# First attention of a two-layer transformer kernel: the fine scores move behind the second values product

## The chip, the cores and the metric

The kernel runs on one core of one Trainium2 chip. Times are device microseconds (us) from the first to the last instruction of that core, as the median of several executions; one profiled execution gives the rows below. PE is TensorE (PEld its weight loads), DVE is VectorE, ACT is ScalarE, POOL is GpSimd, SP is SyncE, which issues most of the DMAs.

## The reference

Two pre-norm layers over 4096 tokens of width 256; only the first attention matters here. Layer norm, three projections, 16 heads of width 16, softmax over all 4096 positions, and an output projection:

```python
def _L0_attn_ref(x, Wq, bq, Wk, bk, Wv, bv, Wo, bo):
    q = _split_heads(x @ Wq.T + bq)
    k = _split_heads(x @ Wk.T + bk)
    v = _split_heads(x @ Wv.T + bv)
    scores = jnp.einsum('hbnd,hbmd->hbnm', k, q) * SCALE
    attn = jax.nn.softmax(scores, axis=-1)
    out = jnp.einsum('hbnm,hbmd->hbnd', attn, v)
    out = jnp.moveaxis(out, 0, 2).reshape(x.shape[0], x.shape[1], DIM)
    return out @ Wo.T + bo
```

Rows of the score matrix belong to keys, the softmax runs over the queries, and the result has one row for each key. Behind it come a two-expert feed-forward layer, a linear attention and a 64-expert mixture, none of which the change touches.

## The kernel before, in words

The function `attention_phase` computes the first attention. Heads go in 8 pairs (`HPAIRS`), two heads beside each other on partitions 0 to 63 and 64 to 127. For each pair the 4096 key columns go in 8 blocks of 512 (`NB`), so there are 64 turns (pair, block), and in a turn the 4096 queries go in 32 chunks of 128 (`MC`).

PE makes four kinds of product, each in a helper:

- `units_a` (line 771): raw scores, keys against 512 queries at a time, both heads, into one of two pairs of banks of `A`. DVE takes the maximum of each (line 882, `PM<-A`). They run one block and 10 units ahead, since a turn's scores need its maxima. It waits for DVE to have emptied the bank pair.
- `unit_s` (line 784): one chunk of one head, 128 queries x 512 keys, with the negated maximum added by extra rows, into one of three banks of `SB`. ACT takes the exponential (line 859, `PR<-SB`).
- `unit_fine` (line 792): the same for the second head's odd chunks, of bf16 parts with 99 rows, as four products of 32 columns, into one bank of `SB`.
- `values` (line 804): `PR` of one chunk, both heads, times the values `VH`, accumulated over the turn in `PV`: four products, each run as two passes of 256 columns, so eight records.

Score number v = 2c + e of a turn (chunk c, head e) takes bank `s_bank(v)`. `unit_s` and `unit_fine` wait until ACT has read what the bank held before (`s_before(v)`). In the rule this is score v - 3; only at the start of a turn the bank order restarts, and score 4 waits for score 3, the one just ahead of it.

PE's function `step` writes one turn out by hand, as 16 iterations of two chunks (q = 2, 4, ..., 32); the scores run two chunks ahead of the values. The order within an iteration is: `units_a`, `unit_s` three times (scores 2q, 2q+1, 2q+2), `units_a`, `values(q-2)`, `unit_fine` (score 2q+3), `values(q-1)`. The third `unit_s`, score 2q+2, waits for the exponential of score 2q-1, which is the preceding iteration's fine score. `values(q-1)` needs that same exponential; `unit_fine` needs the exponential of score 2q.

ACT's function runs `exp` over scores in their order (each waits until PE has made it, and every second one until `values` has freed the buffer of `PR`, of which there are eight), and at a turn's end, behind the exponentials of the next turn's scores 0 to 3, copies `PV` to `OS` (line 870). DVE does the maxima alone, 32 a turn, and one reduction of them. POOL splits the negated maxima into parts, rearranges the keys and issues the stores of `OS`. SP loads keys and queries and places the maxima's parts as rows of `KST` and `KF`. Semaphores count events: `s_done` for finished scores, `s_free` for finished exponentials, `p_free` for finished `values`, `a_done` and `a_free` for raw scores.

Of the kernel before, what the change touches and what calls it, by code (L numbers as in the profile page):

```python
# [112 lines left out]
def count(events):  # L113


    return events + FIRST
# [478 lines left out]
def s_bank(v):  # L595

    return (v if v < 4 else v + 2) % S_BANKS


def s_before(v):  # L600

    for w in range(v - 1, v - EXPS, -1):
        if s_bank(w % EXPS) == s_bank(v):
            return w
# [41 lines left out]
def attention_phase(nc, d, K, V_all, QST, QF):  # L646
# [5 lines left out]
    with ExitStack() as ctx:  # L652
# [35 lines left out]
        def in_steps(eng, body):  # L688

            with eng.Fori(0, HPAIRS // 2) as two:  # L690
                for hp in range(2):
                    for nb in range(NB):
                        body(two, hp, nb)

        def number(two, hp, nb):
            return two * (2 * NB) + (hp * NB + nb)

        sem.start()
        with nc.Block() as block:
# [65 lines left out]
            @block.tensor  # L765
            def _(pe):
                def unit_a(u, e, nb, slot):
                    i, j = divmod(u, NB)
                    rows = slice(e * HALF, e * HALF + STACK)
                    keys = KA[rows, nb % K_SLOTS, i * P:(i + 1) * P]  # L770
                    return nc.tensor.matmul(A[:, u % 2 * 2 + e, :], keys, QST[rows, slot, j * TB:(j + 1) * TB],  # L771
                                            start=True, stop=True)

                def units_a(b, u, nb, slot):
                    pe.wait_ge(a_free, count(b * MC + (u + 1)))
                    first = u % 2
                    unit_a(u, first, nb, slot)
                    unit_a(u, 1 - first, nb, slot).then_inc(a_done, 1)

                def unit_s(t, c, e, nb, slot):  # L780
                    v = 2 * c + e
                    rows = slice(e * HALF, e * HALF + ROWS)
                    pe.wait_ge(s_free, count(t * EXPS + (s_before(v) + 1 + S_BANKS)))
                    nc.tensor.matmul(SB[:, s_bank(v), :], QST[rows, slot, c * P:(c + 1) * P],  # L784
                                     KST[rows, nb % K_SLOTS, :], start=True, stop=True).then_inc(s_done, 1)

                def unit_fine(t, c, nb, slot):
                    v = 2 * c + 1
                    pe.wait_ge(s_free, count(t * EXPS + (s_before(v) + 1 + S_BANKS)))
                    for r in range(4):  # L790
                        at = c // 2 * P + r * 2 * HD
                        mm = nc.tensor.matmul(SB[r * 2 * HD:(r + 1) * 2 * HD, s_bank(v), :],  # L792
                                              QF[0:FINE_ROWS, slot, at:at + 2 * HD],
                                              KF[0:FINE_ROWS, nb % K_SLOTS, :], start=True, stop=True)
                    mm.then_inc(s_done, 1)

                def values(t, c, slot):
                    if c == 0:
                        pe.wait_ge(pv_read, count(t))
                    pe.wait_ge(s_free, count(t * EXPS + (2 * c + 2 + S_BANKS)))  # L800
                    for e in range(2):
                        for b in range(2):
                            at = HALF * e + 2 * HD * b
                            mm = nc.tensor.matmul(PV[at:at + 2 * HD, 0:HB], VH[:, slot, e, c, :],  # L804
                                                  PR[:, (2 * c + e) % P_SLOTS, b * HB:(b + 1) * HB],
                                                  start=(c == 0), stop=(c == MC - 1))
                    mm.then_inc(p_free, 1)

                def step(two, hp, nb):
                    t = number(two, hp, nb)  # L810
                    for q in range(2, MC + 2, 2):
                        ahead, u = divmod(q + LEAD, MC)
                        ahead += 1
                        past, a_nb = divmod(nb + ahead, NB)
                        a_slot = 1 - hp if past else hp
                        if u == 0:
                            pe.wait_ge(ka_ready, count((t + (ahead + 1)) * 2))
                            if a_nb == 0:
                                pe.wait_ge(q_loaded[1 - hp], count((two + (hp + 1) // 2 + 1) * Q_LOAD))
                        s_t, s_nb, s_slot = t, nb, hp  # L820
                        if q >= MC:
                            s_t, s_nb, s_slot = t + 1, (nb + 1) % NB, 1 - hp if nb == NB - 1 else hp
                        if q == MC:
                            block = hp * NB + nb + 1
                            pe.wait_ge(shift_loaded[s_nb % 2], count((two * 8 + (block // 2 + 1)) * SHIFT))
                        units_a(t + ahead, u, a_nb, a_slot)
                        unit_s(s_t, q % MC, 0, s_nb, s_slot)
                        unit_s(s_t, q % MC, 1, s_nb, s_slot)
                        unit_s(s_t, q % MC + 1, 0, s_nb, s_slot)
                        units_a(t + ahead, u + 1, a_nb, a_slot)  # L830
                        if q == 2 and nb == 0:
                            pe.wait_ge(vh_ready, count(two * 4 + (hp * 2 + 2)))
                        values(t, q - 2, hp)
                        unit_fine(s_t, q % MC + 1, s_nb, s_slot)
                        values(t, q - 1, hp)

                pe.wait_ge(q_loaded[0], count(Q_LOAD))
                pe.wait_ge(ka_ready, count(2))
                for u in range(MC):
                    units_a(0, u, 0, 0)  # L840
                pe.wait_ge(ka_ready, count(4))
                for u in range(LEAD):
                    units_a(1, u, 1, 0)
                pe.wait_ge(shift_loaded[0], count(SHIFT))
                units_a(1, LEAD, 1, 0)
                unit_s(0, 0, 0, 0, 0)
                unit_s(0, 0, 1, 0, 0)
                unit_s(0, 1, 0, 0, 0)
                units_a(1, LEAD + 1, 1, 0)
                unit_fine(0, 1, 0, 0)  # L850
                in_steps(pe, step)

            @block.scalar
# [1354 lines left out]
```

## Time and profile before

| what | value |
|---|---|
| median of 3 runs | 4705.39 us |
| lowest and highest run | 4700.58, 4717.93 us |
| span of the profiled execution | 4704.8 us |
| copies of `PV` at the ends of its first and last turn | 305.2 and 2770.9 us |
| PE busy (matmuls) | 4447.2 us, 95% |
| DVE busy | 3534.6 us, 75% |
| ACT busy | 3123.8 us, 66% |
| POOL busy | 853.4 us, 18% |

Besides its span no time of its own is listed for the profiled execution. Busy shares are averages over stages with different limits. Matmuls are pipelined and their recorded ends are modelled, so a busy PE is not PE at its peak; what an engine waited for, and when the next instruction could start, says more.

### The profile page before, as it was taken

The numbers are of one execution on the slowest core, as the hardware profiler recorded it, in microseconds if no ns is written. First come the engines' busy times: TensorE is split into PE (matmuls) and PEld (weight loads), VectorE is DVE, ScalarE is ACT, GpSimd is POOL, SyncE is SP. The second block draws the span as 40 slices with busy tenths as digits, with TensorE's granted clock in tenths as the row PEclk, the third lists the DMA queues.
The fourth block names the chain that finished last, engine by engine and source line by source line (L and its number), as shares of the span: only waits on it lengthen the run. The fifth ranks groups of instructions, "written<-read, shape, count | busy, mean of one in ns | idle before, by whom it ended". The sixth has DMA issues, their size and how long they took to land. (4 is left out here: it accounts for less than half of the span.)

```text
span 4704.8 us, 108333 instructions
## 1 busy us (share of the span) xinstructions
PE 4447.2 (95%) x36787; PEld 2714.8 (58%) x36787; DVE 3534.6 (75%) x3673; ACT 3123.8 (66%) x5610; POOL 853.4 (18%) x1747
## 2 busy tenths in 40 slices
PE   6599999999999999999999969999987699999999
PEld 5344444444444444444444437777866578888887
DVE  4499999999999999999999966555444564545554
ACT  3168888888888888888888855444455454444444
POOL 4311122122111222111211210000000022222222
PEclk8789999999999999999999989999998799999999
DMA  4410110100100101002111130010010422222222
GB/s 160 138 29 13 24 19 13 30 14 13 30 13 18 26 13 30 13 13 66 40 40 40 40 104 27 19 36 27 5 41 27 150 81 87 83 80 86 86 86 87
DMA packets 225729, 229.03 MB, mean 49 GB/s; under 512 B 129665, under 2 KB 169265, under 8 KB 224193
## 3 DMA queue, kind: packets, MB, share of 16 engines
q1 hardware_dynamic: 183936, 146.41, 12.5%
q0 software_dynamic: 41344, 76.61, 5.3%
q8 instruction: 286, 4.69, 0.4%
q14 instruction: 163, 1.33, 0.1%
HBM read 174.41 MB, written 64.55 MB: 51 GB/s over the span
## 5 line engine op out<-in xcount | busy, mean ns | idle before, releaser
L882 DVE TENSOR_REDUCE PM<-A 128x2 f32<-128x1024 f32 x2092 | 2455.3, 1220 | 127.0 <-PE A L771 93.4
L859 ACT ACTIVATE PR<-SB 128x512 f32<-128x512 f32 x4100 | 2121.8, 602 | 374.1 <-PE SB L784 354.5
L804 PE MATMUL PV<-PR,VH 128*32 128x256 f32 x16384 | 1298.5, 387 | 8.1 <-issue 8.1
L771 PE MATMUL A<-QST,KA 48*128 48x512 f32 x4184 | 1196.3, 476 | 59.9 <-DMA QF<-QFD 33.9
L804 PEld LDWEIGHTS PV<-PR,VH 128*32 128x32 f32 x16384 | 434.1, 110 | 562.9 <-issue 374.2
L771 PEld LDWEIGHTS A<-QST,KA 48*128 48x128 f32 x4184 | 430.1, 187 | 521.1 <-issue 413.1
L784 PE MATMUL SB<-KST,QST 50*128 50x512 f32 x3075 | 689.0, 411 | 0.4 <-issue 0.3
L784 PEld LDWEIGHTS SB<-KST,QST 50*128 50x128 f32 x3075 | 388.4, 187 | 205.9 <-ACT PR L859 201.4
L792 PE MATMUL SB<-KF,QF 99*32 99x512 bf16 x4100 | 417.3, 385 | 1.2 <-ACT PR L859 1.2
L2095 DVE TENSOR_TENSOR m_h_lo<-m_h,m_h_hi 128x512 fp32r<-128x512 f32 x320 | 221.2, 691 | 257.3 <-ACT m_h_hi L1990 257.3
L1984 ACT ACTIVATE m_h<-m_h,constants 128x512 f32<-128x512 f32 x320 | 212.4, 664 | 222.4 <-PE m_h L69 220.6
L1990 ACT CAST m_h_hi<-m_h 128x512 fp32r<-128x512 f32 x320 | 188.0, 588 | 247.0 <-DVE m_h L2092 245.0
L1876 POOL DMA_DIRECT2D m_shares<-CW x512 | 264.5, 522 | 442.5 <-DVE m_h L2092 412.0
L2092 DVE TENSOR_TENSOR m_h<-m_h,m_shares 128x512 f32<-128x512 f32 x256 | 178.4, 697 | 190.6 <-ACT m_h L1984 156.1
L954 POOL DMA_DIRECT2D NUM<-OS x256 | 126.0, 492 | 857.3 <-ACT OS L870 795.8
L1254 DVE SCALAR_TENSOR_TENSOR chosen<-gate_out,h_ps 128x512 f32<-128x512 f32 x128 | 88.0, 687 | 194.6 <-PE h_ps L69 194.6
L1193 ACT ACTIVATE h_full<-chosen,constants 128x512 f32<-128x512 f32 x128 | 92.7, 724 | 206.0 <-DVE chosen L1254 205.8
L67 PE MATMUL m_h<-ln_hi,moe_w_hi 128*128 128x512 f32 x512 | 207.0, 404 | 0.0
L67 PE MATMUL m_y<-m_h_hi,moe_w_hi 128*128 128x512 f32 x512 | 202.6, 396 | 3.8 <-DVE m_h_lo L2095 3.4
L68 PE MATMUL m_h<-ln_lo,moe_w_hi 128*128 128x512 f32 x512 | 202.6, 396 | 0.0
L69 PE MATMUL m_h<-ln_hi,moe_w_lo 128*128 128x512 f32 x512 | 202.5, 396 | 0.0
L68 PE MATMUL m_y<-m_h_lo,moe_w_hi 128*128 128x512 f32 x512 | 201.7, 394 | 0.0
(296 smaller groups left out, 5515.6 us busy)
## 6 DMA issues: line engine op xcount, KB each, us to landing
m_shares<-CW POOLq DMA_DIRECT2D x512, 128.0 KB, 2.8
QST<-QS SPq DMA_DIRECT2D x54, 256.0 KB, 8.8
KST<-KS SPq DMA_DIRECT2D x402, 32.0 KB, 1.8
QS<-parts SPq DMA_DIRECT2D x16, 512.0 KB, 3.7
KS<-parts SPq DMA_DIRECT2D x16, 512.0 KB, 2.8
m_x<-X3T SPq DMA_DIRECT2D x16, 512.0 KB, 3.9
moe_w_lo<-W SPq DMA_DIRECT2D x16, 512.0 KB, 10.0
KF<-KFD SPq DMA_DIRECT2D x402, 16.0 KB, 1.7
```

The source lines that it names most:

```text
L67: nc.tensor.matmul(out, w[0], x[0], start=first, stop=False)
L68: nc.tensor.matmul(out, w[0], x[1], start=False, stop=False)
L69: return nc.tensor.matmul(out, w[1], x[0], start=False, stop=last)
L771: return nc.tensor.matmul(A[:, u % 2 * 2 + e, :], keys, QST[rows, slot, j * TB:(j + 1) * TB], start=True, stop=True)
L784: nc.tensor.matmul(SB[:, s_bank(v), :], QST[rows, slot, c * P:(c + 1) * P], KST[rows, nb % K_SLOTS, :], start=True, stop=True).then_inc(s_ ...
L792: mm = nc.tensor.matmul(SB[r * 2 * HD:(r + 1) * 2 * HD, s_bank(v), :], QF[0:FINE_ROWS, slot, at:at + 2 * HD], KF[0:FINE_ROWS, nb % K_SLOTS ...
L804: mm = nc.tensor.matmul(PV[at:at + 2 * HD, 0:HB], VH[:, slot, e, c, :], PR[:, (2 * c + e) % P_SLOTS, b * HB:(b + 1) * HB], start=(c == 0), ...
L859: nc.scalar.activation(PR[:, v % P_SLOTS, :], SB[:, s_bank(v), :], ACT.Exp, scale=SCALE).then_inc(s_free, 1)
L882: nc.vector.tensor_reduce(PM[:, par, :, i, j:j + 1], A[:, u % 2 * 2:u % 2 * 2 + 2, :], AX.X, ALU.max).then_inc(a_free, 1)
L1876: pool.dma_start(shares[e * EH:(e + 1) * EH, p % SHARE_SLOTS, :], d["CW"][2 * p + e, :].partition_broadcast(EH)).then_inc(share_loaded[p % ...
L1984: nc.scalar.activation(h_ps[:, c % RING, :], h_ps[:, c % RING, :], ACT.Silu, bias=bias).then_inc(full_ready, 1)
L2095: nc.vector.tensor_tensor(h[1][:, c % RING, :], h_ps[:, c % RING, :], h[0][:, c % RING, :].bitcast(F32), ALU.subtract).then_inc(lo_ready, 1)
```

## The change

In PE's `step` the second `values` of an iteration is issued ahead of `unit_fine` rather than behind it. Everything else, waits and counts among it, stays as it is.

```diff
                         if q == 2 and nb == 0:
                             pe.wait_ge(vh_ready, count(two * 4 + (hp * 2 + 2)))
                         values(t, q - 2, hp)
+                        values(t, q - 1, hp)
                         unit_fine(s_t, q % MC + 1, s_nb, s_slot)
-                        values(t, q - 1, hp)
```

## Rows read from the trace of the kernel before

**Rows 1.** Busy time by window: start:end, length, PE, PEld, DVE, ACT, POOL, clock, DMA.

```profile
300.00:2780.00 2480.00, 2451.03 (x27274) 1161.85 (x27270) 2383.96 (x2084) 2107.85 (x4106) 483.95 (x1091) 0.99 0.13 26
...
935.00:1205.00 270.00, 269.85 (x3031) 127.83 (x3026) 264.39 (x232) 233.81 (x457) 52.67 (x119) 1.00 0.07 14
```

**Rows 2.** Waits from 300 to 2700 us: total us, times, longest us.

```profile
ACT PR L859 <- PE SB L784: 336.9, 981, 3.8
PEld SB L784 <- ACT PR L859: 193.0, 924, 0.6
...
DVE PM L882 <- PE A L771: 51.7, 79, 4.7
...
PEld A L771 <- DVE PM L882: 34.0, 84, 0.8
```

**Rows 3.** Timeline of DVE: start, length, instruction, count, idle before it and releaser.

```profile
1015.41 21.45 DVE L882 TENSOR_REDUCE PM<-A 128x2 f32<-128x1024 f32 x18 [0.23 <-PE A L771]
```

**Rows 4.** Timeline of the weight loads of one iteration, same columns.

```profile
1014.87 0.19 PEld L771 LDWEIGHTS A<-QST,KA 48*128 48x128 f32 x2 [0.41 <-issue]
1014.98 0.19 PEld L784 LDWEIGHTS SB<-KST,QST 50*128 50x128 f32 x2
1015.40 0.18 PEld L784 LDWEIGHTS SB<-KST,QST 50*128 50x128 f32 x1 [0.23 <-ACT PR L859]
1015.48 0.21 PEld L771 LDWEIGHTS A<-QST,KA 48*128 48x128 f32 x2
1016.06 0.16 PEld L804 LDWEIGHTS PV<-PR,VH 128*32 128x32 f32 x8 [0.37 <-issue]
1016.31 0.12 PEld L792 LDWEIGHTS SB<-KF,QF 99*32 99x32 bf16 x4
1016.52 0.35 PEld L804 LDWEIGHTS PV<-PR,VH 128*32 128x32 f32 x8
1017.28 0.18 PEld L771 LDWEIGHTS A<-QST,KA 48*128 48x128 f32 x2 [0.41 <-issue]
```

**Rows 5.** Timeline of the matmuls of the same iteration: first S, fine, second values.

```profile
1015.21 0.40 PE L784 MATMUL SB<-KST,QST 50*128 50x512 f32 x2
...
1016.52 0.40 PE L792 MATMUL SB<-KF,QF 99*32 99x512 bf16 x4
1016.74 0.62 PE L804 MATMUL PV<-PR,VH 128*32 128x256 f32 x8
```

**Rows 6.** Timeline of ACT: preceding fine exponential; then first, and third with fourth.

```profile
1014.73 0.62 ACT L859 ACTIVATE PR<-SB 128x512 f32<-128x512 f32 x1
...
1015.63 0.60 ACT L859 ACTIVATE PR<-SB 128x512 f32<-128x512 f32 x1 [0.28 <-PE SB L784]
...
1016.60 1.09 ACT L859 ACTIVATE PR<-SB 128x512 f32<-128x512 f32 x2
```

**Rows 7.** Timeline of the first iteration of a turn: copy, loads, second values.

```profile
1012.55 0.40 ACT L870 COPY OS<-PV 128x256 f32<-128x256 f32 x1
1012.74 0.38 PEld L784 LDWEIGHTS SB<-KST,QST 50*128 50x128 f32 x3 [0.28 <-ACT PR L859]
1013.05 0.23 PEld L771 LDWEIGHTS A<-QST,KA 48*128 48x128 f32 x2
...
1014.32 0.62 PE L804 MATMUL PV<-PR,VH 128*32 128x256 f32 x8
```

**Rows 8.** Line 870, once a turn: whole span, and from 930 to 1220 us.

```profile
L870 ACT COPY OS<-PV x64: 403/403/403, 305.2 to 2770.9; 128x256 f32<-128x256 f32 x64
...
L870 ACT COPY OS<-PV x8: 403/403/403, 935.4 to 1205.1; 128x256 f32<-128x256 f32 x8
```

**Rows 9.** Iteration behind a stall: its first and the next A load, and its window.

```profile
892.12 0.29 PEld L771 LDWEIGHTS A<-QST,KA 48*128 48x128 f32 x2 [3.50 <-issue]
...
896.41 0.28 PEld L771 LDWEIGHTS A<-QST,KA 48*128 48x128 f32 x2 [0.81 <-issue]
...
892.10:896.40 4.30, 4.27 (x27) 1.96 (x27) 2.45 (x2) 2.17 (x4) 2.37 (x5) 0.50 0.47 110
```

## The prediction

> **What bounds the kernel now.** I looked first at the busy table by stage. The first attention ends its first turn at 305.2 and its last at 2770.9 us [rows 8]. In it PE is recorded busy nearly all the time and DVE for 264 of 270 us, ACT for 234, at a granted clock of 1.00, the 2.4 GHz level [rows 1]. Matmul ends are modelled, so "busy" does not say that PE is the limit; it only says that three engines run in one loop with little room. The waits say more [rows 2]. In 2,400 us ACT waited 981 times, 0.34 us each, for S scores of PE; the weight load of an S score waited 924 times, 0.21 us each, for ACT's exponential. DVE and PE hardly wait for each other: some 80 times each way. A run of 18 reductions took 21.45 us, 1.19 us each [rows 3]; two of them per iteration are 2.38 us, close to the iteration but not what it waits for.
>
> So I read one iteration (two query chunks), with its loads, matmuls and exponentials [rows 4 to 6]. PE issues: A loads 1014.87, S loads 1 and 2 at 1014.98, S load 3 at 1015.40, the other A loads 1015.48, values 1016.06, fine 1016.31, values 1016.52, next A 1017.28: 2.41 us. The reader should see two things. First, values, fine, values is one stream without a hole: the first values' matmuls start at 1016.06, the fine ones at 1016.52, the second values' at 1016.74 and end at 1017.36. Second, S load 3 stands alone, 0.23 us late. By the code it needs the bank that the previous iteration's fine score filled (the wait of `unit_s` through `s_before`), and ACT finished that exponential at 1014.73 + 0.62 = 1015.35, so 0.05 us before the load. PE takes its waits in order, so the other A loads and the whole values stream stand behind this load.
>
> That makes a loop through both engines, two iterations long: first S end 1015.61, ACT's four exponentials 1015.63 to 1017.69, 0.05 to S load 3, together 2.13; from S load 3 (1015.40) through values, fine, values to the next A load 1.88, from an A load to the end of the first S 0.74. Sum 4.75 for two iterations, 2.38 each. The turn confirms it: seven turns without a stall took 1205.1 - 935.4 = 269.7 us, 38.53 each [rows 8], against 15 x 2.38 plus a boundary iteration of about 2.65, 38.3. In this loop the fine score is not a link: it ends at 1016.92, and ACT, still on the third exponential, takes it only at 1017.69 - 0.62 = 1017.07. It has 0.15 us of room.
>
> **The change, part by part.** No instruction, DMA, buffer or semaphore count is added or removed. Only PE's order changes, in 1,024 iterations (64 turns [rows 8] x 16).
>
> *Second values earlier.* It takes the fine score's slot, about 0.22 us earlier (1016.52 against 1016.74). Its wait needs the exponential of the previous fine score, and S load 3 of the same iteration has waited for that already: no new wait, cost nothing. It frees PR buffers and ends PV earlier. ACT copies PV only after the turn's last fine exponential, so this gains nothing either.
>
> *Fine score later.* It moves behind one values unit: instead of ending at 1016.92 it ends where the stream ends, 1017.36, so 0.44 us later; 0.15 of that is covered. Now the fine score becomes a link of a shorter and slower loop, one iteration long. Nothing in it can run ahead: S load 3 -> other A loads -> values -> values -> fine -> exponential -> next S load 3. Its length:
> - S load 3 to the stream's end: 1017.36 - 1015.40 = 1.96 us [rows 4, 5]. The stream has the same five passes, whatever their order.
> - PE end to ACT start: 1015.61 to 1015.63, 0.02 us, bounds 0.02 and 0.04.
> - Exponential: 0.60 us when ACT comes from idle, 0.62 right behind another one [rows 6].
> - ACT end to weight load: 0.05 us.
>
> That is 2.63 as the rows are rounded; upward rounding of each part gives 2.65; I take 2.64. ACT's other work fits: four exponentials take 2.06 + about 0.5 us of waiting. DVE's 2.38 fits too; it will simply wait. PE's own work is less than the present 2.41.
>
> *Boundary.* In the first iteration of a turn the first S score, not the third, waits for the preceding fine exponential (its bank order restarts). From that load to the stream's end: 1012.74 to 1014.32 + 0.62 = 1014.94, 2.20 us [rows 7]. With the 0.67 to 0.69 of hand-over and exponential that is 2.88. The copy of PV (0.40 us) stands behind the exponential on ACT, while the first S score needs 0.05 + some 0.6 us before ACT can use it: hidden. If it weren't, it would cost 0.4 x 64 = 26 us at most.
>
> *Behind PE.* A waiting S load 3 holds up the other A loads, hence DVE. DVE's maxima come later by the same stretch per iteration, not more; the shift loads, which need the maxima of the next block some six iterations ahead, get proportionally more time. SP and POOL see a slower turn and nothing else: I cost them at nothing, and a miss there would show as a wait at the turn's last iteration.
>
> *Sum.* A turn: 15 x 2.64 + 2.88 = 42.48 us, against 38.53: +3.95. Times 64 = +253 us. The few iterations at half clock and the stalls behind "issue" stay as they are. The profiled span of 4704.8 becomes 4958. The median of the runs, 4705.4, stands 0.6 above this span, so I give 4958.
>
> Bounds of the sum: with the loop at 2.60 (a hand-over hidden) it is 41 us less, at 2.69 (each hand-over longer, exponential 0.62) 51 us more. The case's own range is 4915 to 5010.
>
> **A rule against the rows.** S load 3 was never passed by the other A loads in the iterations read: 1015.40, then 1015.48; at 1012.74 all loads stand behind the first waiting one, and the other A loads come at 1013.05 [rows 4, 7]. The Trainium skill, "TensorE: Matmul & The Clock Gate", section "What a matmul computes" and the table above it, speaks of a partial reorder window that pulls weight loads ahead of matmuls in flight. If that reached past a load that waits for a semaphore, the other A loads (different array rows) could go first and the lateness would be hidden, as in rival 1. The rows speak against that reach.
>
> **Rivals.**
> 1. *Not slower: lateness absorbed* (chance 0.05). If A loads and values passed the waiting S load 3, or if that load waited on something other than the fine exponential, PE would keep its stream and only ACT would shift. Price 0: 4705, within the 0.2% or so by which the runs shown differ. The point that decides: the fine score would have to keep ACT waiting without keeping S load 3 waiting. For it: ACT has 0.34 us of idle per iteration [rows 2] that seems to be free. Against it: that idle lies before the first exponential, not before the fine one, and 924 of some 981 iterations show S load 3 released by ACT.
> 2. *Clock* (0.04). The longer hole before S load 3 could cost the clock. Where PE had stood for 3.5 us, an iteration ran from 892.12 to 896.41, 4.29 us, at 0.50 [rows 9]; that is 1.65 above my 2.64. If one iteration in ten fell to it, +169 us on top: 5127. Against: PE's present holes of 0.4 between loads leave the clock at 1.00 [rows 1, 4], and the new ones are 0.45 long. The same page of the Trainium skill, section "A second HAM failure mode: psum-queue depth-cycling", says that small idles between groups of matmuls can make the clock swing: that would be this rival.
> 3. *Half the price* (0.06). The 0.66 us from S load 3 to the first values were read with the first two S scores still in the array (they end at 1015.61, behind the load at 1015.40 [rows 5]). With the array idle they could be shorter. If S load 3 and what follows came 0.14 us sooner, half of the price would go: -0.14 x 1024 = -143, 4815. Against it: the load itself still has to be made, and it and the other A loads fill most of the 0.66 already.
> 4. The change could only fail to act if the order were not PE's program order. PE runs it in order: excluded but for rival 1.
>
> **Numbers.** Forecast 0.85, rivals 0.05, 0.04, 0.06. Half a per cent, about what a measurement of this kernel tells from no change, is 24 us. Slower by more than that: forecast, rivals 2 and 3, 0.95. Within: 0.04 of rival 1; faster 0.01. The range is the forecast's own, with a little on either side: 4905 to 5015.
>
> **What would show it.** The turn (from copy to copy of PV) at 42.5 us. ACT's waits move: for S scores nearly gone (under 0.1 us each), for the fine score new, about 0.5 us, some 1,000 times. S load 3 waits about 0.45 us for ACT. DVE waits for A in most iterations. Last values row, then fine, then A load in the timeline, still without a hole. Wrong: a turn under 40 us, S load 3 not 0.05 us behind the fine exponential, or a stage clock below 0.97.

## The result, and the profile after

The changed kernel takes 4935.64 us (median of 4 runs, 4929.68 to 4940.22) against 4705.02 for the kernel before in the same rounds: ratio 1.049, 95% interval 1.047 to 1.051, 231 us slower. The forecast was 4958, slower by 253; the measured time lies in its range.

One iteration of the changed kernel, from the timeline of its weight loads, as [rows 4]:

```profile
1012.53 0.19 PEld L771 LDWEIGHTS A<-QST,KA 48*128 48x128 f32 x2 [0.43 <-issue]
1012.63 0.19 PEld L784 LDWEIGHTS SB<-KST,QST 50*128 50x128 f32 x2
1013.29 0.18 PEld L784 LDWEIGHTS SB<-KST,QST 50*128 50x128 f32 x1 [0.47 <-ACT PR L859]
1013.37 0.21 PEld L771 LDWEIGHTS A<-QST,KA 48*128 48x128 f32 x2
1013.95 0.59 PEld L804 LDWEIGHTS PV<-PR,VH 128*32 128x32 f32 x16 [0.36 <-ACT PR L859]
1014.62 0.12 PEld L792 LDWEIGHTS SB<-KF,QF 99*32 99x32 bf16 x4
1015.17 0.19 PEld L771 LDWEIGHTS A<-QST,KA 48*128 48x128 f32 x2 [0.43 <-issue]
```

Its fine matmul, the fine score's exponential (timeline of PE, then of ACT), and the S load 3 of the next iteration:

```profile
1014.84 0.40 PE L792 MATMUL SB<-KF,QF 99*32 99x512 bf16 x4
...
1015.28 0.60 ACT L859 ACTIVATE PR<-SB 128x512 f32<-128x512 f32 x1 [0.41 <-PE SB L792]
...
1015.93 0.18 PEld L784 LDWEIGHTS SB<-KST,QST 50*128 50x128 f32 x1 [0.47 <-ACT PR L859]
```

The whole loop can be read off: S load 3 at 1013.29, fine score done at 1014.84 + 0.40 = 1015.24, 1.95 us later; ACT starts 0.04 behind it and needs 0.60; the next S load 3 comes at 1015.93, 0.05 behind that. 1.95 + 0.04 + 0.60 + 0.05 = 2.64, and 1015.93 - 1013.29 is 2.64. Between the first two S loads and the third, PE's loads now stand still for 0.47 us instead of 0.23 [rows 4].

The waits from 300 to 2700 us, against [rows 2]:

```profile
PEld SB L784 <- ACT PR L859: 420.5, 893, 0.7
...
ACT PR L859 <- PE SB L792: 354.6, 839, 3.8
PEld PV L804 <- ACT PR L859: 301.4, 835, 0.5
DVE PM L882 <- PE A L771: 267.6, 840, 4.0
...
ACT PR L859 <- PE SB L784: 28.6, 63, 2.8
```

ACT's wait has changed its object: 337 us for S scores have become 29, and 355 for the fine score are new. The third S load waits twice as long. DVE, which hardly waited, now waits in most iterations. The 301 us of the values' loads are no new wait, although ACT now stands as their releaser: it is the hole of 0.36 us between the A loads and the values loads, which was 0.37 us and put down to "issue" in the kernel before [rows 4], and the exponential named is the one that S load 3 has already waited for.

The turn, from line 870 over seven turns without a stall and over the whole stage, against [rows 8]:

```profile
L870 ACT COPY OS<-PV x8: 367/367/368, 989.1 to 1286.5; 128x256 f32<-128x256 f32 x8
...
L870 ACT COPY OS<-PV x64: 367/367/368, 304.2 to 3001.7; 128x256 f32<-128x256 f32 x64
```

A turn is (1286.5 - 989.1) / 7 = 42.49 us, against 38.53. From first to last copy it is 2697.5 us against 2465.7, 231.8 more, and that is the whole of the difference in the spans (4935.5 - 4704.8 = 230.7). What lies ahead of the first copy and behind the last one moved by 1 us or less.

### The profile page after: what moved, and what is told of

It reads as the page before. It is cut to its first block and busy times, and to the rows that moved or that the text cites. A ratio compares the mean times of both kernels' runs of the same rounds, so it can differ in the third digit from the quotient of the medians.

```text
span 4935.5 us, 108333 instructions
## 1 busy us (share of the span) xinstructions
PE 4640.7 (94%) x36787; PEld 2702.1 (55%) x36787; DVE 3552.0 (72%) x3673; ACT 3229.2 (65%) x5610; POOL 849.3 (17%) x1747
## 5 line engine op out<-in xcount | busy, mean ns | idle before, releaser
L859 ACT ACTIVATE PR<-SB 128x512 f32<-128x512 f32 x4100 | 2227.8, 598 | 501.9 <-PE SB L792 406.6
L804 PE MATMUL PV<-PR,VH 128*32 128x256 f32 x16384 | 1105.8, 387 | 5.4 <-issue 5.4
L784 PE MATMUL SB<-KST,QST 50*128 50x512 f32 x3075 | 904.8, 431 | 43.4 <-ACT PR L859 16.1
L920 POOL CAST NM<-neg 128x8 fp32r<-128x8 f32 x65 | 12.3, 190 | 1105.9 <-DVE neg L889 1105.9
```

The lines of the kernel that those rows point to most:

```text
L859: nc.scalar.activation(PR[:, v % P_SLOTS, :], SB[:, s_bank(v), :], ACT.Exp, scale=SCALE).then_inc(s_free, 1)
```

## The experiments

Each ratio is against executions of the kernel before in the same rounds; their median was 4705.7 us for the first four experiments, 4710.1 for the next four from `half_exp_before` to `narrow_max_after` and 4702.0 for the last three. The turn is the distance of two copies of `PV` seven turns apart, divided by seven; the last column is how much more the average of all 63 turns is. That excess lies in every eighth turn, where PE's loads stall behind "issue" and the clock mostly falls to half for a while.

| kernel | median us | ratio, 95% interval | copies at | turn us | rest us |
|---|---|---|---|---|---|
| before | 4705.0 | 1 | 935.4, 1205.1 | 38.53 | 0.61 |
| after | 4935.6 | 1.049 (1.047 to 1.051) | 989.1, 1286.5 | 42.49 | 0.33 |
| third_late_after | 4757.2 | 1.012 (1.010 to 1.014) | 941.1, 1217.2 | 39.44 | 0.57 |
| third_late_before | 4738.2 | 1.006 (1.004 to 1.008) | 945.9, 1219.6 | 39.10 | 0.59 |
| fine_first | 4897.1 | 1.040 (1.039 to 1.042) | 981.7, 1274.5 | 41.83 | 0.44 |
| half_exp_after | 4747.2 | 1.008 (1.007 to 1.010) | 940.1, 1214.8 | 39.24 | 0.59 |
| half_exp_before | 4662.1 | 0.989 (0.987 to 0.991) | 920.8, 1186.4 | 37.94 | 0.70 |
| narrow_max_before | 4690.5 | 0.996 (0.994 to 0.998) | 921.4, 1190.2 | 38.40 | 0.69 |
| third_late_narrow | 4668.1 | 0.992 (0.990 to 0.994) | 914.7, 1180.8 | 38.01 | 0.64 |
| narrow_max_after | 4931.4 | 1.048 (1.046 to 1.049) | 985.7, 1283.1 | 42.49 | 0.39 |
| split_raw_before | 4737.8 | 1.008 (1.006 to 1.009) | 941.1, 1214.5 | 39.06 | 0.58 |
| split_raw_after | 4758.6 | 1.012 (1.010 to 1.014) | 945.2, 1221.0 | 39.40 | 0.65 |
| half_exp_narrow | 4643.8 | 0.987 (0.985 to 0.989) | 908.5, 1172.6 | 37.73 | 0.69 |

**Take a stream out of the loop (third_late_after).**

```diff
-                        unit_s(s_t, q % MC + 1, 0, s_nb, s_slot)
                         units_a(t + ahead, u + 1, a_nb, a_slot)
+                        unit_s(s_t, q % MC + 1, 0, s_nb, s_slot)
```

> The changed kernel with its third S score moved behind the second pair of raw scores, so that its load holds up only itself and the values. Loop theory: the second pair of raw scores (two loads and a stream, about 0.21 us) leaves the one-iteration loop; 2.64 becomes 2.43 us, a turn 15 x 2.43 + 2.88 = 39.3 us against 42.47, -3.1 x 64 = -200 us: about 4735 us, ratio to before 1.006. Rival (two values units side by side make the PE stream itself longer, or the fine score last does): PE's work is the same, so 4935 us, 1.049.

Measured: a turn of 39.44, 4757 us. The order values, values, fine was kept, and three quarters of the loss went (the ratio fell from 1.049 to 1.012). So it isn't the order of the last three pieces as such that costs, but what it closes through S load 3. The time is 22 us above the expectation, 9 of it from a longer turn and the rest from the last column of the table. The waits from 300 to 2700 us show that DVE now stands as close as the fine score does:

```profile
PEld A L771 <- DVE PM L882: 218.1, 809, 0.8
...
ACT PR L859 <- PE SB L792: 210.1, 908, 4.3
...
PEld SB L784 <- ACT PR L859: 55.8, 160, 1.2
```

So this run shows that most of the loss goes when a stream leaves the loop; it doesn't show by itself that the fine score's loop is what sets the 39.44 that are left. The run with the shorter exponential below does that.

**The same move in the kernel before (third_late_before).** Same diff.

> The same move in the kernel before. Loop theory: the two-iteration loop of 4.75 us loses 0.21 us and would give 2.27 us an iteration, which is under the pace of PE's own work (four raw and S streams of 0.21, five passes of 0.22, about 0.36 between kinds: 2.30) and of DVE (2 x 1.14 and more): 2.31 us. A turn 37.2 us against 38.53, -1.3 x 64 = -85 us: about 4620 us, ratio 0.982. Rival (the wait of the third S load costs PE nothing now): no change, 4705 us.

Measured: 4738, slower by 0.6%, where I expected 85 us less. The ACT wait did go, as the theory said, but another took its place. Timeline of its weight loads, and two of its waits from 300 to 2700 us:

```profile
1001.66 0.19 PEld L771 LDWEIGHTS A<-QST,KA 48*128 48x128 f32 x2 [0.41 <-issue]
1001.77 0.19 PEld L784 LDWEIGHTS SB<-KST,QST 50*128 50x128 f32 x2
1002.13 0.19 PEld L771 LDWEIGHTS A<-QST,KA 48*128 48x128 f32 x2 [0.17 <-DVE PM L882]
...
1004.02 0.18 PEld L771 LDWEIGHTS A<-QST,KA 48*128 48x128 f32 x2 [0.41 <-issue]
1004.13 0.19 PEld L784 LDWEIGHTS SB<-KST,QST 50*128 50x128 f32 x2
1004.62 0.18 PEld L771 LDWEIGHTS A<-QST,KA 48*128 48x128 f32 x2 [0.30 <-DVE PM L882]
```

```profile
PEld A L771 <- DVE PM L882: 219.6, 795, 0.8
...
PEld SB L784 <- ACT PR L859: 13.6, 60, 0.9
```

There is a second loop, through DVE: from the first A load (1001.66) over its matmul, two maxima and back to the second A load of the next iteration (1004.62) 2.96 us, and from a second A load to the next first one (1002.13 to 1004.02) 1.89; together 4.85 for two iterations, 2.42 each. In the kernel before the second part is 1.80 (1015.48 to 1017.28 [rows 4]). With the S score behind the raw scores DVE must free its banks earlier in the iteration, by as much as PE spends on that S score.

**Fine score ahead of both (fine_first).**

```diff
-                        values(t, q - 2, hp)
                         unit_fine(s_t, q % MC + 1, s_nb, s_slot)
+                        values(t, q - 2, hp)
                         values(t, q - 1, hp)
```

> The kernel before with the fine score ahead of both values units. The fine score's bank comes free when ACT has done the iteration's first exponential. Loop theory: first S end -> exponential and hand-overs 0.67 -> fine load to the next A load 1.22 -> first S end 0.74 is a loop of one iteration, 2.63 us, as long as that of the change by chance; with a boundary of about 2.75 a turn is 42.2 us and the time about 4940 us, 1.05; the waits show the fine score's load waiting for ACT about 0.2 us, 1000 times, and the third S load hardly at all. Rival (only the lateness of the fine score costs, its bank is free anyway): 4705 us or a little less.

Measured: 4897, a turn of 41.83, waits of

```profile
PEld SB L792 <- ACT PR L859: 593.5, 907, 0.7
```

and, in the timeline of its weight loads,

```profile
1001.21 0.10 PEld L792 LDWEIGHTS SB<-KF,QF 99*32 99x32 bf16 x4 [0.66 <-ACT PR L859]
...
1003.82 0.10 PEld L792 LDWEIGHTS SB<-KF,QF 99*32 99x32 bf16 x4 [0.66 <-ACT PR L859]
```

So the fine score must be neither late nor early. It is a different loop than that of the change (the S load 3 does not appear among the twelve longest waits), 2.61 us long where I had worked out 2.63. The wait was mis-sized: 0.65 us each, where I had expected 0.2. The time is 43 us under the expectation, mostly since the turn was 0.4 us shorter than 42.2 and the last column 0.17 less than before. Of the three places tried, the one between the two values units is the one in which its bank is already free and ACT doesn't yet want it.

**Shorten one link (half_exp_after, half_exp_before).** Both leave out half of the fine score's exponential.

```diff
-                    nc.scalar.activation(PR[:, v % P_SLOTS, :], SB[:, s_bank(v), :], ACT.Exp,
+                    n = HB if v % 4 == 3 else TB
+                    nc.scalar.activation(PR[:, v % P_SLOTS, 0:n], SB[:, s_bank(v), 0:n], ACT.Exp,
...
+                nc.gpsimd.memset(PR[:, 3, HB:TB], 1.0)
+                nc.gpsimd.memset(PR[:, 7, HB:TB], 1.0)
```

> The changed kernel with the exponential of the fine score over 256 of its 512 columns alone (the other half of those probabilities is a constant 1). A 256-wide copy on ACT took 0.37 us against 0.60 for the 512-wide exponential, so I expect about 0.39, 0.21 less. Loop theory: it is a link of a one-iteration loop, so every iteration gets 0.21 us shorter: 2.43 us, turn 39.1 us, about 4721 us, ratio 1.003. Rival (PE's stream is what costs): PE's work is the same, 4935 us.

Measured, from the timelines of its weight loads and of ACT (its line numbers are one higher):

```profile
1001.54 0.18 PEld L784 LDWEIGHTS SB<-KST,QST 50*128 50x128 f32 x1 [0.25 <-ACT PR L860]
...
1003.97 0.18 PEld L784 LDWEIGHTS SB<-KST,QST 50*128 50x128 f32 x1 [0.25 <-ACT PR L860]
```

```profile
1001.10 0.39 ACT L860 ACTIVATE PR<-SB 128x256 f32<-128x256 f32 x1 [0.20 <-PE SB L792]
```

The exponential shrank from 0.60 to 0.39 and the iteration from 2.64 to 1003.97 - 1001.54 = 2.43: 0.21 for 0.21. That is what a link of a one-iteration loop does, and DVE is out of the way here: the A loads wait for it 59 times, 21 us in all. The time, 4747, is 26 above the expectation; the turn was 0.14 longer than 39.1, which is 9 us, and the rest is in the last column of the table, which I had carried over from the changed kernel.

> The kernel before with the fine score's exponential 256 columns wide (0.39 us instead of 0.60; the other half of those probabilities is a constant 1). By the loop of my prediction alone (ACT and the third S load, 4.75 us for two iterations) an iteration would fall to PE's own pace, 2.30 us, and the time to about 4620. New theory, from the run with the third S score late: the kernel before has a second loop of the same length, over DVE: A load to its matmul's end 0.50, to DVE 0.04, two maxima 2.36, to the second A load 0.05, from it to the next first A load 1.80, 4.75 us for two iterations. Then only the turn's boundary gains, 0.2 x 64 = 13 us: about 4690 us, ratio 0.997.

Measured: 4662, a turn of 37.94. In the kernel before the same 0.21 us bring about 50 us (1.1%) instead of 188. The time lies between the first reading (4620) and the second (4690). The DVE loop isn't as long as I put it: with S load 3 no longer waiting, the second A load is at 1001.88 and the next first one at 1003.62, 1.74 us and not 1.80, so the loop is 0.50 + 0.04 + 2.36 + 0.05 + 1.74 = 4.69 for two iterations, 2.35. That is also what PE's own work takes (`half_exp_narrow` below), so this run can't tell which of the two holds it. The timeline of its weight loads:

```profile
1001.88 0.19 PEld L771 LDWEIGHTS A<-QST,KA 48*128 48x128 f32 x2
...
1003.62 0.19 PEld L771 LDWEIGHTS A<-QST,KA 48*128 48x128 f32 x2 [0.41 <-issue]
```

**Shorten the maxima (narrow_max_before, narrow_max_after, third_late_narrow).** 64 of each 512 raw scores are left out of the maximum.

```diff
-                            nc.vector.tensor_reduce(PM[:, par, :, i, j:j + 1], A[:, u % 2 * 2:u % 2 * 2 + 2, :], AX.X,
+                            nc.vector.tensor_reduce(PM[:, par, :, i, j:j + 1], A[:, u % 2 * 2:u % 2 * 2 + 2, 0:448], AX.X,
```

> The kernel before with DVE's maxima over 448 of each 512 columns (the other 64 are left out), about 0.13 us shorter each. Two-loop theory: the DVE loop drops to 4.48 us, the ACT loop of 4.75 stays, so an iteration stays at 2.38; only the few iterations in which DVE was late go: 4685 to 4705 us. Rival (DVE alone sets the pace of the kernel before): 2.3 us an iteration or less, about 4620 us.

> The changed kernel with the maxima over 448 of 512 columns. Both theories of mine say that DVE is in no loop that binds here: 2.64 us an iteration, turn 42.5 us, 4935 us, ratio 1.049. If DVE mattered after the change too it would be faster by up to 0.27 us an iteration.

> The kernel before with the third S score late and the maxima over 448 of 512 columns: both loops are shortened. Two-loop theory: 4738 us with the full maxima becomes PE's own pace, 2.31 us an iteration, a turn 37.2 us, about 4620 us, ratio 0.982. Rival (the third S score's own stream is what made that run slower): 4738 us again.

The changed kernel doesn't care (4931, the turn the same 42.49): DVE is in no loop that binds there. The kernel before gains 0.4%, about 20 us, as expected in size, and keeps its wait of S load 3; the waits from 300 to 2700 us:

```profile
DVE PM L882 <- PE A L771: 328.3, 932, 5.2
PEld SB L784 <- ACT PR L859: 203.0, 958, 1.1
```

Little of that gain lies in the loop, though. Its copies of `PV`:

```profile
L870 ACT COPY OS<-PV x64: 406/407/407, 293.4 to 2756.4; 128x256 f32<-128x256 f32 x64
```

From first to last copy it is 2463.0 us against 2465.7 [rows 8], 3 less: the turns without a stall gave 7 us, and the ones with a stall took 4 back. 12 us lie ahead of the first copy (293.4 against 305.2), where the first block's maxima are made; in the runs with full maxima that stretch varied between 298 and 308 us.

The kernel with the S score late drops from 4738 to 4668: it was DVE that had taken the wait over. It was expected at 4620, though. Its turn of 38.01 is not 37.2; the next run shows that PE doesn't run an iteration in 2.30 us.

**How fast PE can go (half_exp_narrow).** Both cuts together, on the kernel before.

> The kernel before with both the 256-wide exponential of the fine score and the maxima over 448 of 512 columns. Neither loop binds; PE's own pace remains, 2.345 us as the last runs show it, boundary 2.44: a turn 37.6 us, with stalls about 4650 us, ratio 0.988. If PE could go faster than that (2.30 us, my earlier estimate), 4615 us.

Measured: 4644, a turn of 37.73. The timeline of its weight loads has neither ACT nor DVE as a releaser; the A loads are 2.35 us apart:

```profile
1000.25 0.18 PEld L771 LDWEIGHTS A<-QST,KA 48*128 48x128 f32 x2 [0.41 <-issue]
1000.35 0.42 PEld L784 LDWEIGHTS SB<-KST,QST 50*128 50x128 f32 x3
...
1002.60 0.19 PEld L771 LDWEIGHTS A<-QST,KA 48*128 48x128 f32 x2 [0.41 <-issue]
...
1004.95 0.19 PEld L771 LDWEIGHTS A<-QST,KA 48*128 48x128 f32 x2 [0.41 <-issue]
```

**An attempt at a faster kernel (split_raw_before, split_raw_after).** Nothing is left out.

```diff
-                        unit_s(s_t, q % MC + 1, 0, s_nb, s_slot)
-                        units_a(t + ahead, u + 1, a_nb, a_slot)
+                        pe.wait_ge(a_free, count((t + ahead) * MC + (u + 2)))
+                        unit_a(u + 1, 0, a_nb, a_slot)
+                        unit_s(s_t, q % MC + 1, 0, s_nb, s_slot)
+                        unit_a(u + 1, 1, a_nb, a_slot).then_inc(a_done, 1)
```

> The order of the kernel before, but the third S score goes between the two raw scores of the second pair: raw (head 0), S score (head 0), raw (head 1), so that the S score streams beside the head-1 raw score as now, yet its load comes one stream (0.21 us) later, when the exponential it waits for is done. Nothing is left out. Loop theory: the ACT loop loses 0.21 us and no longer binds, the DVE loop keeps its 1.74 us from the second raw load to the next first one, 4.69 us for two iterations, 2.35 each, which is also PE's own pace as the last runs show it (2.34 to 2.35). A turn about 38.1 us against 38.53, -0.45 x 64 = -29 us: 4675 us, ratio 0.994. Rival (the second raw pair comes too early for DVE, as in the run with the third S score behind both): 4720 us or more.

> The same in the changed order. One stream leaves the one-iteration loop: 2.64 becomes 2.43 us, a turn 15 x 2.43 + 2.96 = 39.4 us; with the share of stalls seen at this pace (0.57 a turn) about 4755 us, ratio 1.011. If the fine score were no link, 4935 us.

On the changed kernel it does what it should: 4759, near 4755. On the kernel before it is slower, 4738, as the rival said. The second A load comes at 1002.09 and the next first one at 1004.00, 1.91 us, where I had counted on 1.74:

```profile
1002.09 0.27 PEld L771 LDWEIGHTS A<-QST,KA 48*128 48x128 f32 x2 [0.16 <-DVE PM L884]
...
1004.00 0.19 PEld L771 LDWEIGHTS A<-QST,KA 48*128 48x128 f32 x2 [0.41 <-issue]
```

My reading, which no run separates from others: the head-0 raw score no longer streams beside the S score, so a stream lies behind the wait for DVE that lay ahead of it. No kernel that leaves nothing out was faster than the one before.

## Why the prediction was right

*The loop.* The step on which all hangs, that the fine score is no link before and becomes one after, held in its parts: 1.96 from S load 3 to the stream's end was 1.95, the hand-over 0.02 was 0.04, the exponential 0.60 and the last hand-over 0.05 as put; 2.64 came out as 2.64. That it agrees to the last digit is partly luck, since the parts were off by a hundredth or two in opposite directions. The 0.15 us of room and the move of 0.44 need not be added up for that; the loop gives the iteration directly. Two things show it as a loop: a link shortened by 0.21 took 0.21 from the iteration (2.43), and the maxima, outside of it, may shrink without effect. A stream taken out of it (39.44 and 39.40 a turn) agrees, with DVE's loop as long beside it. The signs came as forecast, if smaller: ACT waits for the fine score 0.42 us each, 839 times, where 0.5 us and 1,000 times stood.

*The boundary.* Forecast at 2.88, it can be read off. From the timeline of the weight loads of the changed kernel:

```profile
989.30 0.38 PEld L784 LDWEIGHTS SB<-KST,QST 50*128 50x128 f32 x3 [0.58 <-ACT PR L859]
...
992.17 0.18 PEld L784 LDWEIGHTS SB<-KST,QST 50*128 50x128 f32 x1 [0.46 <-ACT PR L859]
```

From the first S load of the turn to its first S load 3 it is 2.87. With 15 iterations of 2.64 that gives 42.47, and the turn is 42.49, where 42.48 was forecast.

*Second values earlier, cost nothing.* Nothing speaks against it: the stream values, values, fine has no hole (1013.95 to 1015.24), and the copy of `PV` never appears as a wait of PE.

*The sum.* Here is the miss of 22 us. The term is "the few iterations at half clock and the stalls stay as they are". They didn't: in the 63 turns between first and last copy the clean part grew by 3.96 x 63 = 249 us, near the forecast's 253, and the whole by 231.8, so the rest shrank by some 17 us, from 0.61 to 0.33 us a turn. Part of it is the clock. Windows of the kernel before, columns as in [rows 1]:

```profile
595.10:601.90 6.80, 5.90 (x39) 2.80 (x43) 2.45 (x2) 2.25 (x5) 0.00 (x0) 0.50 0.01 4
892.10:902.30 10.20, 10.17 (x61) 5.03 (x61) 5.66 (x5) 4.68 (x9) 2.37 (x5) 0.50 0.86 125
902.30:906.00 3.70, 3.70 (x50) 1.79 (x47) 3.28 (x4) 3.21 (x7) 0.00 (x0) 1.00 0.73 86
...
1523.60:1527.00 3.40, 3.40 (x26) 1.78 (x19) 2.13 (x3) 1.76 (x5) 0.99 (x3) 0.50 0.70 131
```

And of the changed one:

```profile
946.40:949.80 3.40, 3.40 (x27) 1.53 (x19) 2.31 (x3) 1.93 (x4) 1.38 (x3) 0.50 0.54 114
949.80:953.00 3.20, 3.18 (x36) 1.41 (x39) 2.77 (x4) 2.75 (x7) 0.00 (x0) 1.00 0.83 97
...
1308.20:1311.60 3.40, 3.40 (x22) 1.63 (x23) 0.41 (x1) 0.60 (x1) 0.00 (x0) 0.50 0.00 0
```

Between first and last copy each of the two runs at 0.50 (the 1.2 GHz level) six times. In the kernel before these stretches last 3.4 to 10.2 us, 41 us in all; in the changed one each lasts 3.4, 20.5 in all. An iteration at half clock takes 4.29 us [rows 9], so in the kernel before each such microsecond loses 1 - 2.38 / 4.29 = 0.45, and in the changed one 1 - 2.64 / 4.29 = 0.38. That is an estimate of 18 us lost against 8, so the clock accounts for about 10 of the 17. Another 4 or so lie in the stalls themselves: the holes of over 1.2 us in PE's loads add up to 20.0 us in the kernel before and to 15.8 in the changed one. The last column of the table tends to fall as the turn gets longer, from 0.69 at 37.7 us to 0.33 and 0.39 at 42.5, and the time at half clock tends to fall with it, from 51 us in that run to 20.5 and 24. How long PE had stood doesn't tell the two kernels apart at the stall that ends a pass of PE's loop: 3.50 us without a load before 892.12 [rows 9], 3.44 before 944.93, and 10.2 us at half clock behind the one against 3.4 behind the other. In the changed kernel the clock fell even behind a shorter hole:

```profile
1308.11 0.18 PEld L804 LDWEIGHTS PV<-PR,VH 128*32 128x32 f32 x8 [1.93 <-issue]
```

Why the stretches and the holes are shorter was not tried and stays open.

*What bounds the kernel before.* This part was right in kind and too simple. The loop of 4.75 us over ACT is there, but PE's own pace is 2.35 and the DVE loop 2.35 to 2.38, so three limits lie within 0.03 us. I had written that DVE is "not what it waits for": true of the waits, but it stands just behind, which is why moving S load 3 out of ACT's way, behind the raw scores that DVE waits for, made the kernel slower. My expectation for PE's own pace, 2.30, was an addition of streams and was 0.05 too short. The sum for the change didn't use either, since it took the turn before as measured.

*The rivals.* That a waiting S load is passed: no, it is held 0.47 us, and the other A loads follow 0.08 us behind it (1013.29, 1013.37). The Trainium skill says that loads are pulled ahead of matmuls in flight ("TensorE: Matmul & The Clock Gate", the table above the section "What a matmul computes"). The rows agree in that loads start while matmuls run: the A load of 1015.17 starts before the fine matmuls end at 1015.24. Past a load that waits for a semaphore none went in the iterations read. The clock: 1.00 in the iterations read and in the window from 950 to 1305 us,

```profile
950.00:1305.00 355.00, 349.11 (x3616) 151.89 (x3615) 317.47 (x276) 292.42 (x543) 63.95 (x142) 1.00 0.14 21
```

with holes of 0.47 us in the loads of each iteration read. Half the price, because the array is idle when S load 3 comes: the 0.66 from there to the first values was again 0.66 (1013.29 to 1013.95).

## What to carry to other kernels

In an order written out by hand, follow each buffer's reuse around the iteration until it closes, count how many iterations the loop spans, and compare its length per iteration with each engine's own work; in this kernel each move within PE's stream cost or gained through the loops that it lengthened or shortened, also those of engines that it didn't touch. Idle time on an engine (0.34 us of ACT here) is room only for what can use it at that place. Before taking out the wait that shows, work out the next-longest loop, because one that is nearly as long hardly shows in the list (34 us for DVE in the kernel before [rows 2], 220 once S load 3 had moved).

## What the runs showed that I had not expected

The kernel before sits at a point where ACT's loop, DVE's loop and PE's own pace are 2.38, 2.35 to 2.38 and 2.35 us an iteration; shortening ACT's alone gave 1.1%, DVE's alone 0.4% (most of it ahead of the loop), both 1.3%, and two moves meant to relieve ACT cost 0.6 and 0.8%. The time at half clock in the first attention was 41 us in the kernel before, in stretches of 3.4 to 10.2 us, and 20.5 us in the slower one, where every stretch was 3.4.
